# Projecting raw transposed activations, with the mean of the first norm subtracted inside the open banks

## What is computed

```
x = x + attn(layernorm(x))        # Wqkv 1024x768, one head of 256, softmax, Wo 256x1024, bo
x = x + fake_quant(layernorm(x)) @ fake_quant(ctx)      # ctx is 1024x1024 for each batch
x = x + ffn(layernorm(x))         # 3584 hidden units in 56 blocks of 64, one unit picked in each block

def _layernorm(x, axis=-1, eps=1e-05):
    m = jnp.mean(x, axis=axis, keepdims=True)
    v = jnp.var(x, axis=axis, keepdims=True)
    return (x - m) / jnp.sqrt(v + eps)
```

## Time and profile before

| what | value |
|---|---|
| median of 3 executions | 773.01 us (772.47 to 773.91) |
| the profiled execution, its own time | 772.67 us |
| its span | 770.9 us |
| PE busy / DVE / POOL / ACT, share of the span | 99% / 79% / 63% / 31% |
| granted TensorE clock | 1.0 in every slice |
| first transpose of xn on PE | 9.40 us |
| first transpose of the probabilities (PT 0 0), on the chain | 88.19 us |
| first add_XA on DVE | 131.15 us |

### The profile page before, as it was taken

The page is one execution under the profiler, slowest core; times in us unless marked ns, Lnnn a source line. Parts: engine busy times, 40 slices in busy tenths (PEclk is TensorE's granted clock), DMA queues, the critical chain, the costliest instruction groups (busy, mean ns, idle before and its releaser), DMA issues.

```text
span 770.9 us, 11315 instructions
## 1 busy us (share of the span) xinstructions
PE 763.4 (99%) x3610; PEld 627.0 (81%) x3614; DVE 610.2 (79%) x964; ACT 242.3 (31%) x368; POOL 484.0 (63%) x306
## 2 busy tenths in 40 slices
PE   8999999999999999999999999999999999999998
PEld 7888887478888888888888888888888888888887
DVE  6888769987884878888878788787888887778864
ACT  6347668763321130312122221303031212222120
POOL 4878898767999974645637363636464563736360
PEclk9999999999999999999999999999999999999999
DMA  9526406300211111222222221212222222222114
GB/s 326 200 109 218 169 18 148 61 2 7 63 54 62 53 57 50 69 75 68 75 68 68 68 75 63 71 40 61 56 68 75 68 75 68 68 68 68 61 37 195
DMA packets 57463, 63.70 MB, mean 83 GB/s; under 512 B 39136, under 2 KB 41440, under 8 KB 57184
## 3 DMA queue, kind: packets, MB, share of 16 engines
q1 hardware_dynamic: 57152, 62.22, 25.9%
q10 hardware_dynamic: 288, 1.18, 0.4%
HBM read 50.79 MB, written 4.19 MB: 71 GB/s over the span
## 4 chain that ended last, share of the span: by engine, by line
PE 93%; DVE 4%; DMA 1%; ACT 1%; issue 1%; SPq 0%; DVEq 0%; ACTq 0%
PE bank L1895 13%; PE bank L1896 13%; PE bank L1897 13%; PE bank L1789 12%; PE bank L1790 12%; PE bank L1791 12%; PE bank L1598 4%; PE bank L1600 4%; PE bank L1599 4%; PE bank L1780 2%; DVE x L1270 1%; DMA x<-x_in 1%; PE bank L1759 1%; DVE xn L1251 1%; PE bank L1741 1%; PE bank L1614 1%
## 5 line engine op out<-in xcount | busy, mean ns | idle before, releaser
L1895 PE MATMUL bank<-w_hi,h_hi 128*128 128x512 f32 (+1 forms) x450 | 175.5, 390 | 0.0
L1896 PE MATMUL bank<-w_lo,h_hi 128*128 128x512 f32 (+1 forms) x450 | 175.3, 390 | 0.0
L1897 PE MATMUL bank<-w_hi,h_lo 128*128 128x512 f32 (+1 forms) x450 | 174.7, 388 | 0.0
L1390 DVE TENSOR_TENSOR x<-bank,x 128x512 f32<-128x512 f32 x207 | 132.8, 685 | 48.2 <-PE bank L1897 48.2
L640 POOL TENSOR_TENSOR lo_r<-r,slot 128x512 fp32r<-128x512 f32 x52 | 68.2, 1313 | 141.8 <-ACT slot L879 141.8
L1897 PEld LDWEIGHTS bank<-w_hi,h_lo 128*128 128x128 f32 x450 | 84.5, 188 | 18.0
L1895 PEld LDWEIGHTS bank<-w_hi,h_hi 128*128 128x128 f32 x450 | 84.5, 188 | 17.1
L1896 PEld LDWEIGHTS bank<-w_lo,h_hi 128*128 128x128 f32 x450 | 84.7, 188 | 15.0
L1789 PE MATMUL bank<-xT_hi,slot 128*128 128x512 f32 x240 | 93.7, 390 | 0.0
L1790 PE MATMUL bank<-xT_lo,slot 128*128 128x512 f32 x240 | 93.4, 389 | 0.0
L1791 PE MATMUL bank<-xT_hi,lo_r 128*128 128x512 f32 x192 | 74.7, 389 | 0.0
(11 more groups left out here) (214 smaller groups left out, 1587.1 us busy)
## 6 DMA issues: line engine op xcount, KB each, us to landing
r<-w SPq DMA_DIRECT2D x56, 256.0 KB, 3.5
w_raw<-w SPq DMA_DIRECT2D x28, 512.0 KB, 3.9
x<-x_in SPq DMA_DIRECT2D x8, 512.0 KB, 10.7
ctx_raw<-ctx_in SPq DMA_DIRECT2D x8, 512.0 KB, 3.7
xn<-ctx_in SPq DMA_DIRECT2D x8, 512.0 KB, 4.6
out<-x SPq DMA_DIRECT2D x7, 512.0 KB, 2.7
W_raw<-wqkv SPq DMA_DIRECT2D x6, 512.0 KB, 10.4
xT_raw<-xT_in SPq DMA_DIRECT2D x1, 2048.0 KB, 19.7
```

The source lines that it names most:

```text
L1390: nc.vector.tensor_tensor(x[:, t, c], bank[unit_banks(g)[p]][:, :], x[:, t, c], ALU.add).then_inc(unit_added, 1)
L1895: nc.tensor.matmul(dst, h_hi[:, j, m], w2_hi[:, j, c], start=j == 0, stop=False)
L1896: nc.tensor.matmul(dst, h_hi[:, j, m], w2_lo[:, j, c], start=False, stop=False)
L1897: last = nc.tensor.matmul(dst, h_lo[:, j, m], w2_hi[:, j, c], start=False, stop=j == GJ - 1)
```

## The change

- The high and low parts of the projections' moving operand are cut from **raw** x, transposed on the host for both batches (`xT_in` now holds both). The transposes of the first norm (T1), the `norm` calls of round 0, `norm_xT` and the R jobs are gone. `WARM` is 18.
- The four Q jobs of batch 0 come first, all four banks open at once, in five chunks of the contraction (`K_CHUNKS`), each as soon as its part of x and W has landed.
- Subtracting the mean: `(x - m) W = x W - m * sum(W)`. The column sums of W are read off a transposed copy of the weights (`wT_in`, 3 MB more to load): columns 0 and 1 by ScalarE, the others by VectorE's `sum_W`. `split_w_cols`, `split_m_cols` cut sums and means in hi and lo, `spread_weight_sums` and `spread_rows` transpose them into 4 rows, ScalarE copies these to SBUF, and `centre_qk` / `centre_v` add one matmul with 4 rows of contraction to each open bank (8 of 512 columns, 8 of 256).
- Dividing by s: `scale_Q` on VectorE multiplies each Q bank by `rstd_row`, 8 new operations of 128x512. For V it is in the operation that adds the bias.
- The hand-written orders change: the attention's jobs, the loads (x 4 to 7 last), and the places of `scale_ctx`, `round_ctx`, `convert_ctx`, `cut_Wo` and `add_q2`.

```diff
-WARM = 44
+WARM = 18
@@ job_order
-    jobs = both("T1", 0) + both("T1", 1) + both("T1", 2) + [("V", 0, 0)] + both("T1", 3)
-    jobs += [("V", 0, 1), ("Q", 0, 0), ("R", 0), ("Q", 0, 1), ("R", 1), ("Q", 0, 2), ("Q", 0, 3), ("V", 1, 0)]
+    jobs = [("Q", 0, c) for c in range(4)] + [("V", 0, 0), ("V", 0, 1)]
     jobs += [("S", 0, i) for i in range(4)]
-    jobs += [("Q", 1, c) for c in range(4)] + [("V", 1, 1)]
+    jobs += [("V", 1, 0)] + [("Q", 1, c) for c in range(4)] + [("V", 1, 1)]
@@ gpsimd
             convert_ctx(0, 1)
+            add_bo(5)
+            convert_ctx(2, 3)
             add_bo(6)
-            convert_ctx(2, 3)
+            convert_ctx(4, 5)
             add_bo(7)
-            convert_ctx(4, 5, 6, 7)
+            convert_ctx(6, 7)
             add_q2(0, 1)
             convert_ctx(8, 9, 10, 11)
             add_q2(0, 2)
             add_q2(0, 3)
-            convert_ctx(12, 13, 14)
+            cut_Wo()
             add_q2(0, 4)
-            convert_ctx(15)
-            cut_Wo()
+            convert_ctx(12, 13, 14, 15)
             add_q2(0, 5)
@@ scalar
             act.dma_start(Wo_raw[:, :, :], wo).then_inc(Wo_loaded, 16)
             hi_V(1, 1)
+            scale_ctx(11)
             for i in range(TB):
                 hi_PT(0, i)
@@ vector: new functions
+            def sum_W(i):
+
+                dve.wait_ge(wT_loaded[i], 16)
+                nc.vector.tensor_reduce(wsum[:, DC * i:DC * i + DC], wT[:, DC * i:DC * i + DC, :], AX.X,
+                                        ALU.add).then_inc(kv_wsummed, 1)
+            def scale_Q(b, c):
+
+                dve.wait_ge(mm_done, nth("Q", b, c) + 1)
+                dve.wait_ge(rows_copied, 2 * b + 1)
+                nc.vector.tensor_tensor(job_bank("Q", b, c)[:, :], job_bank("Q", b, c)[:, :], rstd_row[:, :],
+                                        ALU.mult).then_inc(q_scaled, 1)
@@ vector: order
+            scale_Q(0, 0)
+            scale_Q(0, 1)
             lo_Q(0, 0)
-            norm_xT(0)
+            scale_Q(0, 2)
             lo_Q(0, 1)
-            norm_xT(1)
+            scale_Q(0, 3)
+            sum_W(2)
+            split_w_cols(slice(4, 6))
             lo_Q(0, 2)
+            lo_Q(0, 3)
...
-            lo_Q(0, 3)
+            lo_V(0, 0)
+            lo_V(0, 1)
+            first_stats(4)
+            first_stats(5)
+            maxima(0)
+            first_stats(6)
+            first_stats(7)
+            split_m_cols(1)
+            norm_scale(0, 4)
@@ tensor: new functions
+            def spread_weight_sums(i):
+
+                pe.wait_ge(w_cols_ready, i + 1)
+                if i == 1:
+                    pe.wait_ge(rows_copied, 1)
+                home = rows_bank[0] if i else job_bank("V", 0, 1)
+                for n in range(2 if i else 4):
+                    last = nc.tensor.transpose(home[0:4, n * P:(n + 1) * P], w_cols[:, 4 * i + n, :].bitcast(F32), id_f[:, :])
+                last.then_inc(w_spread, 1)
+            def centre_qk(b, c):
+
+                pe.wait_ge(w_copied, 1)
+                pe.wait_ge(rows_copied, 2 * b + 2)
+                nc.tensor.matmul(job_bank("Q", b, c)[:, :], w_rows[0:4, c * P:(c + 1) * P], m_rows[0:4, :], start=False,
+                                 stop=True).then_inc(mm_done, 1)
@@ tensor: order
+            project_v(0, 0, with_q_sums)
+            project_v(0, 1, with_v_sums)
+            centre_v(0, 0)
+            centre_v(0, 1)
             for i in range(TB):
                 scores(0, i)
+            project_v(1, 0)
+            project_qk(1, 0, with_rows)
+            project_qk(1, 1, with_centring)
```

More of the change, by code:

```diff
@@ new lines, in sum_W, with copy_w_rows @@
+            def sum_W(*columns):
+                for j in columns:
+                    act.wait_ge(wT_loaded[j // DC], 16)
+                    nc.scalar.activation(wT[:, j, :], wT[:, j, :], ACT.Copy,
+                                         accum_out=wsum[:, j:j + 1]).then_inc(q_wsummed, 1)
+            def copy_w_rows(i):
+                act.wait_ge(w_spread, i + 1)
+                if i == 0:
+                    act.wait_ge(W_lo_done, VALUE_CHUNK)
+                    nc.scalar.activation(w_rows[0:4, :], job_bank("V", 0, 1)[0:4, :], ACT.Copy).then_inc(w_copied, 1)
+                else:
+                    nc.scalar.activation(wv_rows[0:4, :], rows_bank[0][0:4, 0:HD], ACT.Copy).then_inc(w_copied, 1)
@@ L1051, in _ @@
             hi_u(0)
-            both(hi_T, 2, 6)
-            both(hi_T, 2, 7)
+            both(hi_T, 6)
+            both(hi_T, 7)
             hi_w2(0, 0)
@@ L1152, in norm_scale, with lo_T @@
                                                    ALU.mult).then_inc(rstd_ready, 1)
-            def lo_T(rnd, t, halves=(0, 1)):
-                for h in halves:
-                    job = ("T1" if rnd == 0 else "T3", t, h)
+            def lo_T(t):
+                for h in range(2):
+                    job = ("T3", t, h)
                     dve.wait_ge(hi_done, nth_hi(*job) + 1)
```

590 lines of the change are left out of this document (319 added, 271 removed).

## The result

The changed kernel takes 786.16 us (median; 785.06 to 787.12) beside 773.30 us (772.47 to 773.91) for the kernel before: a ratio of 1.017 (95% interval 1.0157 to 1.0182), slower by 13 us. The forecast was 781.3 with a range up to 786.0, so the sign was right, and the time lies 4.9 us above the forecast and 0.16 us outside the range. The profiled execution took 786.98 us with a span of 785.2, 14.3 more than the span of before; the other executions took 785.06 to 787.12.

The account below looks back on a forecast made before the run. TensorE was busy 99% of the span, but GpSimd's list was taken to decide, starting the first `add_XA` 8.6 us later: 772.67 + 8.6 = 781.3 us, range 775.5 to 786; TensorE's start gain was nearly used up by waits.

Parts of the forecast that it names:

- PT starts at 87.5: TensorE's first transposed probability of batch 0: start forecast at 87.5, 0.7 earlier than before (87 to 89.5).
- GpSimd's term: GpSimd's list from ctx 11's conversion (95.4) to the first `add_corr` (139.8): `add_XA(0)` 8.6 us later; 65%.
- `ones_r` over 3 us: Sign of being right: VectorE's `ones_r` waits out GpSimd's cut of Wo and lasts over 3 us.
- signs of being wrong: PT before 85, a cut of Wo ending before 102, or a first `add_corr` behind which VectorE is late.
- The rows of batch 1: TensorE's wait for VectorE's `rstd` before spreading these rows: ready at 59.7, up to 62; wait 1.4 us (to 3.7).
- The centring: TensorE's added 4-row matmuls that subtract the mean: priced as full matmuls, 0.228 us each at 512 columns.
- The clock: TensorE's clock falls to 1.2 GHz when idle ahead of the output projection: about 1.3 us, left out of the sum.
- WO: Output projection on TensorE: WO (0, 0) starts at 107.1 to 109.3 instead of 102.65, 4.5 to 6.6 late.
- Worse: Rival: both TensorE waits at their long end, VectorE 3 us late into PT, GpSimd adding that: 786; 7%.
- The start: TensorE's first projection begins at about 4.95 instead of 9.40: 4.45 us gained.
- the start is gained: Rival: both TensorE waits vanish, GpSimd has served additions and conversions by PT, PT at 82.7: 767.2; 11%.
- waits only: Rival: GpSimd catches up through faster additions; only WO's late start of 4.5, less VectorE's slack, stays: 776.5; 12%.

Follow-up runs that it names:

- e1: Kernel before, with its old start, given only the changed kernel's late ctx tiles in the three lists: 783.06 us (772.93 before).
- e8: Changed kernel with weight sums taken, and loaded, over 64 of the 1024 rows only: 782.69 us (772.97 before).
- e6: Changed kernel with 18 transposes nobody reads ahead of TensorE's wait for `rstd` of batch 1: 785.71 us (772.97 before).
- e3: Changed kernel with VectorE's `ones_r` and the round of ctx 13 moved behind the two `lo_O` of batch 0: 786.66 us (772.93 before).
- e5: Changed kernel with batch 1's rows spread in Q (1, 1), centring in Q (1, 2), `sum_W(2)` ahead of the first scaling: 783.86 us (772.97 before).
- e16: e13 with GpSimd's additions of ctx 2 and 3 moved behind the cut of Wo: 779.58 us (773.27 before).
- e13: e12 with rounds of ctx 12 and 13 behind `lo_PT` and GpSimd's three additions ahead of conversions 12 to 15: 776.04 us (773.29 before).
- e10: Changed kernel with `sum_W(2)` early, batch 1's statistics ahead of maxima, ctx tiles earlier, conversions ahead of Wo's cut, `ones_r` behind `lo_O`: 779.71 us (773.06 before).
- e7: e5 with the whole order of the ctx tiles as in the kernel before, scalings and rounds moved forward to match: 785.16 us (772.97 before).
- e11: e10 with round 12 ahead of V (1, 1), 13 behind `lo_PT`, and tiles 0 to 5 and the bias additions moved: 778.80 us (772.97 before).
- e12: Changed kernel with TensorE's order of e5, ctx lists moved forward, bias additions one by one between conversions: 776.62 us (772.91 before).
- e14: e13 with each ctx tile brought one place forward, rounds 2 and 3 ahead of `norm_scale`: 777.12 us (773.29 before).
- e15: e13 with two of GpSimd's additions (ctx 2 and 3) done on 8 of 1024 columns: 775.81 us (773.27 before).
- e2: Changed kernel with the late ctx tiles moved forward again, two conversions and three additions ahead of the cut of Wo: 782.12 us (772.93 before).
- e4: Changed kernel with batch 1's rows after all of Q (1, 0) on TensorE and the centring after Q (1, 1): 784.01 us (772.93 before).

## Why the prediction was right in kind and 4.9 us short

**What failed is the size of the term "PT starts at 87.5".** The mechanism was the one forecast, GpSimd's late list; PT came at 91.96, the conversion of ctx 11, put at 95.4, ended at 99.5, and that carried the time just past the range's end of 786. Of the 4.9 us most are this term: e1, whose conversion of ctx 11 ends at 95.35 as forecast, took 783.06, so about 3.1 come with the late PT, and 1.8 are in GpSimd's term and behind it; e8, with PT at 87.28, took 782.69. Of the forecast's signs of being right, PT at 87 to 89, `ones_r` over 3 us and the first `add_XA` near 140 (144.97) didn't come; none of its signs of being wrong did. Three parts add up to the 4.5 us.
- *The rows of batch 1*, forecast for 59.7, came at 61.27: 1.6, still inside the bound of 62. Of this, 0.4 was there at TensorE's first projection (5.33 for 4.95); and the eight operations on single numbers, taken at 1.5, took 3.0, since one of them lasted 2.36.
- *The centring.* From the rows to PT the forecast had 27.8; e6, with the clock at 1.00, took 29.1 (60.69 to 89.77). 1.3: a centring matmul of 512 columns that stands alone starts 0.43 ahead of the next matmul, where I had taken 0.228. Only the four in a row (x4 in 1.19) come near the price that I took for all. On the chain the eight of batch 1 make 2.4 us for the 1.4 taken.
- *The clock*: 30.7 in the changed kernel against 29.1 in e6, 1.6. The forecast had considered a fall of the clock ahead of WO, priced it at 1.3 and left it out; it had none for the wait at 60. Ahead of WO it fell as well (0.50 from 112 to 116), behind 5.48 us of idle time; what that costs the whole can't be read off, since GpSimd is later still.

The sum itself has a slip: 59.7 and its parts 1.0, 2.7 and 22.9 make 86.3, not 87.5. By its own parts the forecast of PT was 5.7 short and not 4.5, and 1.2 of that was made good by the slip, which is luck. Luck is also that the rival *Worse* named the time, 786: it wanted both waits of TensorE at their long end (the second up to 3.7), and they were 1.7 and 2.2. Only its third condition held, VectorE 3 us late at PT (`v_lo` of V (1, 1) at 93.62 for 89.59).

**GpSimd's term** was nearly right. From the end of that conversion to the start of the corrections the list took 42.6 us; the forecast's 95.4 and 139.8, less 2.5 for one correction, leave 41.9. That GpSimd has no gap from the conversion of ctx 15 on held, and `add_XA(0)` came 13.8 later, not 8.6: 4.1 by the conversion, the rest by the cuts (5.04 for 4.62, 1.74 for 1.29) and the round that fell into the first correction. e1 is the term by itself: PT where it was, `add_XA` 9.3 later (forecast 8.6), 10.1 us slower. e3, e5 and e16, where `add_XA(0)` waits 3.6 to 5.7 us for GpSimd, show that it sets the end.

**WO.** Forecast 107.1 to 109.3, measured 112.81. I had the 0.95 of waiting for Wo's high part as saved; ScalarE waited 4.04 us for the load of Wo instead, which took 8.62 us against 5.2 before. `ones_r` took 2.43, not over 3; the round behind it bore the cut. The idle time of more than 4.5 ahead of WO was right (5.48).

**The start.** The wait for the weight sums was forecast as 2.0 and was 1.7; `sum_W(2)` took 2.28 (forecast 2.4). The gain of the start was real, and e13 shows that most of it can be kept up to PT (2.9 earlier than before). The rival *the start is gained* fell all the same, for the reason given there: ctx 11 can't be converted ahead of PT. The rival *waits only* fell with e1. The loads of 3 MB, costed at nothing, held nobody (under e8). What stands behind the first `add_XA` added 0.5 us (14.3 at the end, 13.8 at `add_XA`); TensorE waits 1.2 us there for the load of a quantised operand (`q1T`), which it did not before.

**Rule and row.** A round takes 0.72 us free; behind GpSimd's cut of Wo it took 4.50 (e1) and 4.89 (e3), and two of them beside two additions 4.32 (e10). By the Trainium skill ("SBUF — State Buffer", "Who interferes with whom") a copy, cast or tensor_scalar of VectorE in its fast mode waits out GpSimd's running instruction, and these rows agree. The granted clock was 0.50 in the changed kernel behind 2.15 and behind 5.48 us of idle time. That an idle TensorE falls to 1.2 GHz is what the Trainium skill has ("TensorE: Matmul & The Clock Gate", "What's actually happening"); these two waits agree, and some others, listed at the end, show no fall.

**What stays open.** Rewriting the lists took back 10 of the 13 us, and no arrangement came under the kernel before, though e7, e10, e11, e12 and e14 were each expected to come level with it or under it. So that the lists cost most of the 13 us is shown; that the new projections leave VectorE room enough, so that some list would cost nothing, is not, and the rival of those runs (no room) is neither shown nor ruled out for the last 3 us. In e13 GpSimd is done with its additions at 91.85 and waits 0.71 for the round of ctx 12; e15 takes the additions away and gains nothing. So two bounds lie within a microsecond of each other there, GpSimd's work and the time at which VectorE gets to the rounds of 12 to 15; no run relaxed both at once. In e2 and e4 it isn't separated how much the late load of Wo adds.
